# Adding the attention mask inside VectorE's maximum instead of with a TensorE matmul

## What is computed

```python
# causal attention: B 2, L 2048, D 256, 16 heads of 16, 4 key heads (each shared by 4 heads)
sc = jnp.einsum('bhqd,bhkd->bhqk', q, k) / jnp.sqrt(jnp.float32(dh))
mask = jnp.where(jnp.tril(jnp.ones((L, L), bool)), 0.0, -1000000000.0)
p = jax.nn.softmax((sc + mask).astype(jnp.float32), -1).astype(q.dtype)
o = jnp.einsum('bhqk,bhkd->bhqd', p, v).transpose(0, 2, 1, 3).reshape(Bsz, L, D)
...
# band attention: 16 heads of 16, |query - key| <= half, half at most 60
band = jnp.abs(idx[:, None] - idx[None, :]) <= half
scores = jnp.where(band[None, None], scores, -1e+30)
attn = jax.nn.softmax(scores, axis=-1)
```

## Time and profile before

| what | value |
|---|---|
| median of 3 runs | 4175.17 us (4169.05 to 4177.55) |
| the profiled execution's own time | 4178.09 us |
| its span, first to last instruction | 4176.3 us |
| mean granted TensorE clock | 0.927 of 2.4 GHz |
| causal attention, first to last of its attention work | about 1165 to 2345 us |
| band attention | about 3265 to 3870 us |

### The profile page before, as it was taken

One profiled execution on the slowest core, in us unless ns is written; L12 is line 12 of the kernel. 1 busy time (PEld: TensorE's weight loads), 2 busy tenths in 40 slices (PEclk: granted clock), 3 DMA queues, 4 the chain that ended last, 5 costly groups with the idle time before them and its releaser, 6 DMA issues. The chain is left out here.

```text
span 4176.3 us, 47591 instructions
## 1 busy us (share of the span) xinstructions
PE 3479.3 (83%) x17329; PEld 1741.4 (42%) x17329; DVE 2425.5 (58%) x4104; ACT 1680.8 (40%) x2670; POOL 1143.2 (27%) x975
## 2 busy tenths in 40 slices
PE   6889999986579989999899799938883778778799
PEld 2334433332233333333333265614551455456465
DVE  2999999999457767677677133265613233344212
ACT  4655555554214545555555412111122334334222
POOL 2667677667321001220000000001222223211000
PEclk9999999999879999999999899969996889889799
DMA  2222222222231111211120100021222854653100
GB/s 78 71 67 70 68 69 68 67 69 72 51 59 35 22 30 32 41 36 29 28 37 7 46 16 10 5 97 56 70 71 86 150 95 91 120 82 51 32 15 20
DMA packets 210060, 232.04 MB, mean 56 GB/s; under 512 B 58695, under 2 KB 160408, under 8 KB 208524
## 3 DMA queue, kind: packets, MB, share of 16 engines
q1 hardware_dynamic: 206764, 220.72, 23.0%
q0 software_dynamic: 3072, 8.39, 0.6%
HBM read 183.13 MB, written 45.89 MB: 55 GB/s over the span
## 5 line engine op out<-in xcount | busy, mean ns | idle before, releaser
L1365 DVE TENSOR_REDUCE g_mxp<-PS 128x1 f32<-128x512 f32 (+3 forms) x1280 | 722.6, 606 | 222.2 <-PE PS L1511 122.0
L1237 ACT ACTIVATE g_pT<-PS 128x1024 f32<-128x1024 f32 (+3 forms) x640 | 552.4, 894 | 474.6 <-PE PS L1526 279.1
L379 POOL TENSOR_TENSOR WB<-m_dtx,WB 128x1024 f32<-128x1024 f32 x256 | 601.0, 2351 | 294.3 <-DVE WB L523 260.1
L411 ACT ACTIVATE PS<-m_dt,m_A 128x512 f32<-128x512 f32 x512 | 353.1, 691 | 431.0 <-DVE WB L514 430.4
L1503 PE MATMUL PS<-g_KT,WB 96*128 96x512 bf16 (+3 forms) x1280 | 429.3, 363 | 105.9 <-DVE g_mxp L1365 92.9
L608 PE MATMUL PS<-WB,ident 128*128 128x512 f32 x1024 | 503.0, 615 | 0.0
L514 DVE TENSOR_TENSOR_SCAN WB<-PS,m_state,WB 128x512 f32<-128x512 f32 x384 | 469.9, 1263 | 14.9 <-ACT PS L411 14.8
L1526 PE MATMUL PS<-WB,g_KT 99*128 99x512 bf16 (+3 forms) x1280 | 358.1, 352 | 1.2 <-ACT g_pT L1237 0.6
L1503 PEld LDWEIGHTS PS<-g_KT,WB 96*128 96x128 bf16 x1280 | 116.9, 98 | 480.6 <-DVE g_mxp L1365 400.9
L523 DVE TENSOR_TENSOR WB<-WB,PS 128x1024 f32<-128x1024 f32 x256 | 306.2, 1196 | 7.2 <-DVE WB L514 2.6
L1545 PE MATMUL PS<-g_pT,WA 128*32 128x512 f32 (+3 forms) x2560 | 300.9, 542 | 0.6 <-ACT g_pT L1237 0.6
(11 more groups left out here) (309 smaller groups left out, 5360.2 us busy)
## 6 DMA issues: line engine op xcount, KB each, us to landing
WB<-b_rows SPq DMA_DIRECT2D x256, 256.0 KB, 3.2
WB<-in_L_ffn_w SPq DMA_DIRECT2D x18, 1024.0 KB, 7.6
WB<-g_dq SPq DMA_DIRECT2D x96, 128.0 KB, 3.9
WB<-w_dq SPq DMA_DIRECT2D x96, 128.0 KB, 7.7
w_KT<-w_dk SPq DMA_DIRECT2D x96, 128.0 KB, 8.4
g_rden<-g_dn SPq DMA_DIRECT2D x128, 64.0 KB, 2.0
w_dv<-WA SPq DMA_DIRECT2D x8, 1024.0 KB, 4.7
w_V<-w_dv SPq DMA_DIRECT2D x16, 512.0 KB, 12.1
```

Source lines behind the costliest of these rows:

```text
L379: pool.tensor_tensor(hh[:, g % RING, :, :], dtx[:, MB * h:MB * h + MB, :], Bs[:, g % BRING, :].unsqueeze(1) .broadcast_to([P, MB, CH]), AL ...
L411: act.activation(PS[:, 2 + b, :], dt[:, c % 2, m, :], ACT.Exp, scale=Aneg[:, n, m:m + 1]).then_inc(dA_ready, 1)
L1237: act.activation(pT[:, n % 2, 2 * pair:2 * pair + 2, 0:width], PS[:, 2 * pair:2 * pair + 2, at:at + width], ACT.Exp, scale=DH ** -0.5).the ...
L1365: dve.tensor_reduce(mxp[:, q % 6, i % QB, hh:hh + per, k0 // CH if causal else 0], PS[:, 4 + m % 2, :].rearrange("p (h n) -> p h n", h=per ...
```

## The change

The 1024 mask matmuls of the max steps (L1511; 512 in each attention) are gone. VectorE adds the mask in the instruction that takes the maximum: `tensor_tensor_reduce` reads the scores from PSUM and the mask from SBUF, writes the sum back over the scores and accumulates the maximum. It takes one head at a time, so a band step, which was one instruction for two heads, has two calls. Each call is two VectorE instructions: one over the scores, and one that writes the accumulated maximum to `mxp`. The causal mask tile becomes 512 columns wide with 384 zeros ahead of the diagonal square, filled once by a memset. The mask matmuls of the turn steps stay, and so do the 768 causal steps without a diagonal. The list of steps is not touched.

```diff
-            mask_q = sb(tag + "_mq", [P, P], BF16)
+            mask_q = sb(tag + "_mq", [P, CH], BF16)
...
+                if causal:
+                    chain(dve.memset(mask_q[:, 0:CH - P], 0.0))
...
                     if what == "max":
-                        m, q, hh, (i, k0, width, *_) = x
+                        m, q, hh, (i, k0, width, m0, m_width, m_at) = x
                         dve.wait_ge(mx, m + 1)
-                        dve.tensor_reduce(
-                            mxp[:, q % 6, i % QB, hh:hh + per, k0 // CH if causal else 0],
-                            PS[:, 4 + m % 2, :].rearrange("p (h n) -> p h n", h=per)
-                            [:, :, 0:width], AX.X, ALU.max).then_inc(mx_read, 1)
+                        scores = PS[:, 4 + m % 2, :].rearrange("p (h n) -> p h n", h=per)
+                        at = k0 // CH if causal else 0
+                        if m_width:
+                            if causal:
+                                m_at = CH - width
+                            for e in range(per):
+                                ins = dve.tensor_tensor_reduce(
+                                    out=scores[:, e, 0:width], in0=scores[:, e, 0:width],
+                                    in1=mask_q[:, m_at:m_at + width], scale=1.0, scalar=-3e38,
+                                    op0=ALU.add, op1=ALU.max,
+                                    accum_out=mxp[:, q % 6, i % QB, hh + e, at:at + 1])
+                            ins.then_inc(mx_read, 1)
+                        else:
+                            dve.tensor_reduce(mxp[:, q % 6, i % QB, hh:hh + per, at],
+                                              scores[:, :, 0:width], AX.X, ALU.max)\
+                                .then_inc(mx_read, 1)
...
-                                               start=(lo == k0), stop=not m_width,
+                                               start=(lo == k0), stop=hi == k0 + width,
...
-                            if m_width:
-                                mm = pe.matmul(bank[:, m0:m0 + m_width], k.identb[:, :],
-                                               mask_q[:, m_at:m_at + m_width],
-                                               start=False, stop=True, skip_group_check=True)
```

More of the change, by code:

```diff
@@ L1000, in _ @@
                     weight(v_w, "v_w")
-                    load(mask_q[:, :], a["c_mask_q"])
+                    load(mask_q[:, CH - P:CH], a["c_mask_q"])
                     load(mask_k[:, :], a["c_mask_k"])
@@ L1486, in _ @@
                     if what == "max":
-                        m, q, hh, (i, k0, width, m0, m_width, m_at) = x
+                        m, q, hh, (i, k0, width, *_) = x
                         s, J, g = block_of(q)
```

## The result

| | before | after |
|---|---|---|
| median | 4176.36 us (4169.05 to 4188.65, 6 runs) | 4156.84 us (4143.21 to 4163.30, 6 runs) |
| ratio | 1 | 0.9947, 95% interval 0.9926 to 0.9968 |
| span of the profiled execution | 4176.3 us | 4153.6 us |
| causal attention, first score matmul to end of last output projection | 1180.1 us | 1170.4 us |
| band attention, the same | 618.7 us | 598.4 us |

The kernel is 19.5 us faster, 0.5%. In the profiled pair the band attention gives 20.3 us and the causal one 9.7; some 7 us come back outside them (the stretch between the attentions went from 914.3 to 920.5 us), where no instruction was changed. Single executions differ by that much: in the 13 traces of this document the time outside the two attentions lies between 2372 and 2390 us. The band's 618.7 us run to the last output projection, some 14 us beyond the end that the opening table gives.

What follows compares the result with a forecast made beforehand. TensorE was the fuller engine (83% busy, VectorE 58%), trading pace with VectorE in the causal attention and waiting for transfers in the band one. 4178.1 - 1 causal - 29 band = 4148 us, written as 4147; range 4122 to 4186.

Steps and rivals of the forecast that it cites:

- The forecast case: Whole kernel: nearly all of the gain in the band attention, -29 us, and -1 us causal; chance 0.68.
- TensorE's masks, causal: Causal attention: 512 mask matmuls removed, 30 us at most, of which a cautious 50% shows, 15 us.
- VectorE's part, causal: Causal attention: the second VectorE instruction lengthens masked steps, costing 14 us where the maximum holds TensorE.
- The price of 0.09 us: VectorE: time the new second instruction adds to each masked step, bounded by small instructions at 0.07 and 0.19 us.
- The share of 30%: Causal attention: share of steps where a longer maximum holds TensorE, taken between 12% and 50%.
- VectorE's part, band: Band attention: last maximum of each of 32 blocks ends 0.26 us later and starts the late row chain, 8 us.
- 63 us in the band attention: Band attention: TensorE time of the removed masks, 55.6 us at full clock, 63 us at the granted 0.88.
- the cover: Band attention: 31% of TensorE's work precedes late transfers, so 43 of 63 us show; against that 8 and 6 us.
- 7 fixed pieces of 8 us: Band attention: TensorE work ahead of the seven waits for the maxima's rows, where removed masks gain nothing, 56 us.
- Rival 2: Band attention: waits for transfers grow by what TensorE saves, leaving about -5 us in all, 4170; chance 0.15.
- Rival 3: Band attention: granted clock falls from 0.88 to 0.84, costing 23 us and leaving about -6, 4169; chance 0.05.
- Rival 1: Causal attention: VectorE becomes the pace, kernel slower if the second instruction costs from 0.20 us; 4204 at 0.25; chance 0.12.

Runs made afterwards that it cites:

- e4: Kernel before plus VectorE adding the mask in both attentions while TensorE keeps its mask matmuls, so the mask counts twice in the maximum; 4188.12 us, 1.0027 of before.
- e3: Changed kernel with plain maxima of unmasked scores, nobody masking the max steps, and the causal exponential's scale divided by 65536; 4143.72 us, 0.9923 of before.
- the square: Kernel before, changed kernel, e3 and e4 compared: TensorE's masks kept or gone, VectorE's sum present or absent; causal attention 1180.1, 1170.4, 1160.9 and 1191.3 us.
- e7: Changed kernel plus a memset of 128 fp32 columns on VectorE ahead of each of the 512 masked causal sums; 4176.61 us, 1.0003 of before.
- e2: Kernel before with the change made in the causal attention alone, the band attention left as it was; 4176.69 us, 0.9987 of before.
- e6: Changed kernel with the two small DMAs of the maxima's rows moved from SyncE's queue to ScalarE's in the band attention; 4116.42 us, 0.9862 of before.

## Why the prediction was right, and where it was off

The measured 4156.84 us lies 10 us above the 4147 forecast, on the side forecast, and the ratio's interval excludes 1. The forecast case is the one that came: the band attention carries most of the gain. That the sum came so close is partly luck. The two stages together gave 30.0 us in the profiled pair, exactly the 30 forecast, but the causal one gave 8.7 more than forecast (9.7 for 1) and the band one 8.7 less (20.3 for 29). The 10 us by which the time missed are not in the stages: some 7 of them are time outside the attentions, which no term covered and no run explains.

**TensorE's masks, causal.** Predicted gain 15 us of 30; measured 19 to 21. About two thirds of the removed time shows, not half.

**VectorE's part, causal.** Predicted cost 14 us; measured 9.5 and 11.2. The price of 0.09 us was too high: the second instruction adds 0.01 between starts and 0.07 until the maximum is told, and VectorE's busy time in the stage grew by 24.5 to 28.1 us wherever VectorE took over the sum (given pair; before and e4; e3 and the changed kernel), 0.05 a masked step. In the square 34 to 40% of that shows. The share of 30% was thus not far off, though e7 leaves it at about 40 to 60%. The net, -1 predicted, is -5 us by e2's times and -9.7 by the given pair of traces.

**VectorE's part, band.** Predicted 8 us from a row chain that starts later; measured 3 at most (e3, e4). A band step costs 0.76 us in bursts, not 0.88. TensorE's waits for the maxima themselves grew from 1.0 to 4.7 us; why no more of it reached the chain of the rows isn't shown.

**The failed term: 63 us in the band attention.** I took the masks at the mean clock of the window, 0.88, as if low-clock time would shrink with the work. As a price of what stood there that was right: in the trace before, the 512 masks take 63 us between starts. (The 0.112 and 0.085 us are the distances in the trace at full clock; by columns alone, 256 / 2.4, it would be 0.107, and the text of the prediction mixes the two.) But the low level stands at the waits, and the waits stayed, so it fell on other matmuls. Low-clock working time went from 92 to 106 us, and work fell by 47.1 us and not by 63. That is 15.9 us too much. On the other side the waits grew by 26.8 us where I had 20 for the cover, 8 and 6, together 34: 7.2 too many. Work and waits make up the stage, so the difference, 8.7, is what the band's -29 misses its -20.3 by: again two errors that partly cancel. The 20 us of cover were not far off in size, but not in their make-up: I had counted 7 fixed pieces of 8 us for the rows, but the waits for `w_dm` grew by only 4.1 us, those for `On` by 8.0 and those for `V` by 9.1. In this stage a saved microsecond showed up in whatever transfer was next due.

**Rivals.** Rival 2 (the transfers take all) had the right mechanism with 27 of 47 us, not all. Rival 3 (the clock falls from 0.88 to 0.84) did happen, 0.87 to 0.83, at a chance of 0.05, but it cost about 7 us (half of 14.6) and not my 23: I charged the mean clock to all of the work, while nearly half of the low level lies in the waits (93 of 199 us). Its place was beside the forecast and not against it. Rival 1 didn't happen. Its threshold was of the right size: its sum puts the second instruction at 0.17 us for a kernel that gains nothing, and e7 gains nothing with 0.13 us a step added to VectorE's busy time.

**Marks in the profile.** Sum instruction 0.71 and 0.44 us for 0.69 and 0.42: right. The next one 0.07 to 0.1 behind: the read ends 0.06 behind the sum, but the next sum follows at once. VectorE busy up by 110 to 200: it was 64, since the read overlaps the next sum. Causal within 5 us of 1180: it came down by 9.7. The band stage came down by 20 and not 29. Waits for `w_dm` and `w_On` up by 10 to 20: 12.1 together.

**A better version.** e6, the changed kernel with the rows' DMAs on ScalarE's queue in the band attention, is the fastest kernel here that leaves nothing out: 4116.42 us, 0.9862 [0.9848, 0.9876].

## What to carry to other kernels

Price an added VectorE instruction twice: what it adds to the distance between starts, and what it adds until the result is told; and test how much of it shows by adding one more, whose price you read from start to start in that run's own trace, with the instructions on both sides of it: here the memset's own start-to-start distance was half of what it added to a burst. Where an engine waits for transfers, work taken off it is worth only what no transfer takes back: ask which transfers come due next, and time both versions with those transfers left out. Price removed matmuls at the full clock unless the waits that bring the clock down go with them. When a stage is cut in idle time and work, count both from the same instruction.

## What the runs showed of the hardware

- The read of an accumulated maximum is an instruction of its own, 141 ns long. The next sum starts 0.01 us behind its start, a memset 0.10 us behind it (e7).
- The sum and maximum with its result written back to PSUM lasts 711, 571, 439 and 305 ns over 512, 384, 256 and 128 columns; the plain maximum lasts 685 and 418 ns over 512 and 256. These are means, and the length depends on what runs ahead: over 512 columns the sum lasts 0.70 us where VectorE was idle ahead of it (the plain maximum 0.69), 0.73 behind a read and 0.67 behind e7's memset. So the 26 ns between the means are no price of writing 512 columns to PSUM.
- A memset of 128 fp32 columns lasts 0.17 us, and the sum behind it starts 0.08 us behind its start; put between two sums of a burst, it moved them from 0.62 to 0.77 us apart.
- In the band attention TensorE's granted clock fell to its low level 32 times in the two given traces, 31 of them during a long wait of TensorE or within 1 us of one.
- TensorE filled with useless matmuls in its waits made the kernel before faster, 0.9972 [0.9960, 0.9983] (e8), with the band's granted clock at 0.94 instead of 0.87.
